# Attention walks: a written-out order of heads and steps for the first three and the last three walks, the periodic order only between them

## Time and profile before

| | |
|---|---|
| runs shown | 1484.58, 1487.13, 1488.78 us, median 1487.13 us |
| profiled execution | 1487.57 us, of it the span 1485.6 us |
| PE busy | 1411.2 us (95%), DVE 1124.7 (76%), ACT 1062.7 (72%), POOL 700.3 (47%) |
| granted PE clock, mean | 0.98 |
| chain that ended last | PE 87%, DVE 5%, issue 2%, ACT 2%, POOL 2%, DMA 2% |

### The profile page before, as it was taken

How to read it: one execution, slowest core, us unless ns; L and a number is a source line. 1 busy time by engine, 2 the same in 40 slices (tenths; PEclk the granted TensorE clock), 3 DMA queues, 4 the chain that set the end, 5 groups by cost and what they waited for, 6 DMA issues and landing times.

```text
span 1485.6 us, 38191 instructions
## 1 busy us (share of the span) xinstructions
PE 1411.2 (95%) x15004; PEld 1137.8 (77%) x15004; DVE 1124.7 (76%) x1991; ACT 1062.7 (72%) x2144; POOL 700.3 (47%) x619
## 2 busy tenths in 40 slices
PE   5689999999999999999999999999987999999996
PEld 3458888888888888898888889798874556767666
DVE  5578999999999999999999999999856621312215
ACT  6467878888787888878788887878654646465551
POOL 0535555455455555445554544555315535354440
PEclk9789999999999999999999999999998999999998
DMA  3000102021110202111020212202042111212100
GB/s 117 1 1 24 39 22 58 9 52 30 30 37 24 58 8 53 27 34 37 23 58 2 59 23 38 37 24 44 9 107 47 54 36 37 72 36 72 36 1 29
DMA packets 100999, 55.90 MB, mean 38 GB/s; under 512 B 74572, under 2 KB 93016, under 8 KB 100824
## 3 DMA queue, kind: packets, MB, share of 16 engines
q1 hardware_dynamic: 100824, 53.47, 15.1%
HBM read 35.62 MB, written 1.05 MB: 25 GB/s over the span
## 4 chain that ended last, share of the span: by engine, by line
PE 87%; DVE 5%; issue 2%; ACT 2%; POOL 2%; DMA 2%; POOLq 0%; SPq 0%; DVEq 0%; ACTq 0%
PE bank L387 11%; PE bank L1341 11%; PE bank L1324 10%; PE bank L542 6%; PE bank L588 5%; PE bank L529 5%; PE bank L559 4%; PE bank L577 4%; PE bank L568 3%; PE bank L469 3%; PE bank L477 3%; PE bank L485 3%; PE bank L437 2%; PE bank L413 2%; PE bank L438 2%
## 5 line engine op out<-in xcount | busy, mean ns | idle before, releaser
L878 DVE SCALAR_TENSOR_TENSOR con<-bank,taps,con 128x1022 f32<-128x1022 f32 (+2 forms) x192 | 245.2, 1277 | 13.2 <-ACT con L657 8.6
L1663 POOL TENSOR_TENSOR h<-h 128x512 f16<-128x512 f32 x120 | 142.5, 1192 | 159.8 <-ACT h L1441 147.4
L1034 POOL TENSOR_TENSOR gl<-const_sb,gc 128x512 f16<-128x512 f32 x128 | 129.7, 1040 | 141.7 <-DVE gc L888 84.3
L387 PE MATMUL bank<-x,qkv 128*128 128x512 f16 x768 | 184.6, 392 | 10.5 <-DVE con L878 10.2
L1440 ACT ACTIVATE h<-bank,b 128x512 f32<-128x512 f32 x120 | 82.5, 688 | 119.2 <-PE bank L1324 116.2
L1324 PE MATMUL bank<-y,w 128*128 128x512 f16 x720 | 162.8, 385 | 1.9 <-ACT h L1441 1.4
L1341 PE MATMUL bank<-w,h 128*128 128x256 f16 x1440 | 160.0, 273 | 0.0
L1341 PEld LDWEIGHTS bank<-w,h 128*128 128x128 f16 x1440 | 140.8, 98 | 18.5
L387 PEld LDWEIGHTS bank<-x,qkv 128*128 128x128 f16 x768 | 73.3, 100 | 93.1 <-issue 12.9
L936 DVE TENSOR_TENSOR X<-X,bank 128x512 f16<-128x512 f16 x192 | 129.3, 680 | 14.4 <-PE bank L477 12.7
L1324 PEld LDWEIGHTS bank<-y,w 128*128 128x128 f16 x720 | 70.1, 99 | 90.5 <-ACT h L1441 8.2
(11 more groups left out here) (221 smaller groups left out, 3927.8 us busy)
## 6 DMA issues: line engine op xcount, KB each, us to landing
w<-in_w SPq DMA_DIRECT2D x24, 640.0 KB, 4.5
w_qkv<-in_W_qkvz SPq DMA_DIRECT2D x16, 512.0 KB, 3.9
w_z<-in_W_qkvz SPq DMA_DIRECT2D x16, 256.0 KB, 2.8
w_out<-in_W_out SPq DMA_DIRECT2D x16, 256.0 KB, 3.0
Z<-in_xT SPq DMA_DIRECT2D x2, 512.0 KB, 5.4
y<-in_x SPq DMA_DIRECT2D x1, 1024.0 KB, 7.8
sqo<-oo SPq DMA_TRANSPOSE x64, 3.1
out_dram<-y SPq DMA_DIRECT2D x8, 128.0 KB, 1.8
```

Source lines behind the costliest of these rows:

```text
L387: last = mm(bank[:, b], qkv16[:, w, a, t * P:(t + 1) * P], x16[:, x, a, b * S:(b + 1) * S], start=(a == k == 0), stop=(a == HT - 1 and k = ...
L878: stt(out=out, in0=bank[:, 0:B, 0:S - k], scalar=taps[:, par, t, TAPS - 1 - k:TAPS - k], in1=out, op0=ALU.mult, op1=ALU.add).then_inc(tap_ ...
L1034: last = tt(gl[:, g % 2, k].rearrange("p (m r) d -> p m r d", m=2), upper.unsqueeze(1).unsqueeze(1).broadcast_to([P, 2, R, P]), gc[:, par, ...
L1663: tt(h16[:, n % 2, 1, t, at], h32[:, k % H32], h16[:, n % 2, 0, t, at], ALU.subtract).then_inc(h_low, 1)
```

## The change

The walks -2, -1 and 0 become one written list `FIRST` of 306 entries (head, step, x), the walks 13, 14 and 15 one written list `LAST` of 370. Between them walks 1 to 12 (`MIDDLE`) stay as they were. Both lists hold the same entries as the walks that they replace: no step is added or dropped, only the order differs. `steps_of` with its special case is gone, `run` goes through one list `STEPS`, and `place` looks up the use's number in it. The banks of `BANK` stay, but the order of the uses of a bank follows the lists. The banks in which the gate matmuls work change from (4, 2) to (3, 2).

```diff
-GATE_BANKS = (4, 2)
+GATE_BANKS = (3, 2)
+FIRST = [
+    (0, "load", "qkv"), (0, "split", "qkv"), (0, "proj", 1), (0, "tap", 1),
+    (0, "load", "out"), (0, "silu", 1), (0, "tap", 2), (0, "tok", 0),
+    (0, "tok", 1), (0, "proj", 2), (0, "tap", 3), (0, "sq1", 1),
+    (0, "gc", 0), (0, "proj", 3), (0, "kT", 0), (0, "gl", 0),
+    (0, "silu", 2), (0, "gl", 1), (0, "v", (0, 1)), (0, "v", (0, 0)),
+    (0, "tap", 0), (0, "silu", 3), (1, "load", "qkv"), (0, "proj", 0),
+    (0, "decay", 0), (0, "kd", 0), (0, "silu", 0), (0, "decay", 1),
+    (0, "kk", 0), (0, "sq", 0), (0, "gl", 2), (0, "aT", 0),
+    (0, "kk", 1), (0, "kT", 1), (0, "gl", 3), (0, "aH", 0),
+    (0, "aT", 1), (0, "aH", 1), (0, "kk", 2), (0, "st", 0),
...
+    (1, "silu", 1), (0, "split", "out"), (0, "norm", 0), (1, "proj", 2),
...
+    (0, "res", 0), (0, "y", (5, 1)), (1, "v", (0, 0)), (0, "split", "z"),
+    (1, "silu", 3), (1, "proj", 0), (0, "p", (5, 1)), (1, "tap", 0),
+    (0, "once", 0), (0, "res", 1), (0, "turn", (5, 1)), (1, "gl", 3),
+    (0, "res", 2), (0, "Z", 0), (0, "once", 2), (0, "once", 1),
+    (2, "load", "qkv"), (1, "load", "z"), (1, "silu", 0), (0, "res", 3),
+    (1, "decay", 1), (1, "v", (1, 1)), (1, "kk", 0), (1, "aT", 0),
...
+LAST = [
...
+    (14, "z", 1), (14, "weigh", 0), (15, "y", (4, 1)), (14, "high", 0),
+    (14, "weigh", 1), (15, "pT", 3), (15, "p", (5, 0)), (15, "v", (1, 0)),
+    (15, "turn", (3, 1)), (14, "z", 2), (15, "p", (4, 1)), (14, "high", 1),
+    (14, "z", 3), (14, "weigh", 2), (15, "y", (5, 1)), (15, "turn", (4, 1)),
+    (15, "turn", (5, 0)), (15, "res", 0), (14, "high", 2), (15, "p", (5, 1)),
+    (15, "res", 1), (15, "once", 0), (14, "op", 0), (15, "once", 1),
+    (15, "turn", (5, 1)), (15, "Z", 0), (14, "weigh", 3), (14, "oT", 3),
+    (15, "oT", 0), (14, "high", 3), (15, "res", 2), (14, "power", 0),
+    (15, "oT", 1), (14, "op", 1), (14, "low", 0), (15, "once", 2),
+    (14, "op", 2), (15, "Z", 2), (14, "low", 1), (15, "Z", 1),
+    (15, "kd", 1), (15, "oT", 2), (15, "solve", 0), (14, "op", 3),
+    (15, "su", 0), (15, "res", 3), (15, "ks", 1), (15, "pdl", 0),
+    (15, "solve", 1), (15, "qs", 1), (15, "su", 1), (15, "once", 3),
+    (15, "pdl", 1), (15, "sqo", 0), (15, "sqo", 1), (15, "sum", 0),
+    (15, "ks", 2), (14, "low", 2), (15, "split", "out"), (15, "Z", 3),
...
+MIDDLE = range(1, NK - 3)
+STEPS = FIRST + [(w + a, step, x) for w in MIDDLE for a, step, x in ORDER if 0 <= w + a < NK] + LAST
+USES = {b: [(n, step, x) for n, step, x in STEPS if BANK.get((step, x)) == b] for b in range(2, 8)}
+PLACE = {use: (b, k) for b in range(2, 8) for k, use in enumerate(USES[b])}
```

More of the change, by code:

```diff
@@ L106 @@
 }
-GATE_BANKS = (4, 2)
-DEEP = max(a for a, *_ in ORDER)
-AHEAD = {(step, x): a for a, step, x in ORDER}
-TILES = (1, 2, 3, 0)
[L115 to L130, removed]
@@ L131 @@
-STARTS = {(b, w): sum(len(USES[b, i]) for i in range(-DEEP, w)) for b in range(2, 8) for w in range(-DEEP, NK)}
-def place(n, step, x):
[L136 to L140, removed]
+GATE_BANKS = (3, 2)
[7 more added lines that the diff above has]
+    (0, "decay", 0), (0, "kd", 0), (0, "silu", 0), (0, "decay", 1),
[14 rows of a table added]
+    (0, "turn", (1, 1)), (1, "proj", 1), (0, "p", (2, 1)), (0, "turn", (3, 0)),
+    (0, "y", (4, 0)), (1, "tap", 1), (0, "turn", (2, 1)), (1, "gl", 1),
+    (1, "gl", 2), (1, "decay", 0), (0, "p", (4, 0)), (0, "y", (3, 1)),
+    (1, "silu", 1), (0, "split", "out"), (0, "norm", 0), (1, "proj", 2),
+    (0, "y", (5, 0)), (0, "p", (3, 1)), (1, "sq1", 1), (1, "tap", 2),
+    (1, "tok", 0), (1, "tok", 1), (0, "pT", 3), (1, "load", "out"),
+    (0, "turn", (4, 0)), (0, "aL", 2), (0, "turn", (3, 1)), (1, "silu", 2),
[4 rows of a table added]
+    (1, "silu", 3), (1, "proj", 0), (0, "p", (5, 1)), (1, "tap", 0),
+    (0, "once", 0), (0, "res", 1), (0, "turn", (5, 1)), (1, "gl", 3),
+    (0, "res", 2), (0, "Z", 0), (0, "once", 2), (0, "once", 1),
+    (2, "load", "qkv"), (1, "load", "z"), (1, "silu", 0), (0, "res", 3),
[10 rows of a table added]
+    (0, "pdl", 1), (1, "aL", 1), (1, "turn", (0, 0)), (0, "sqo", 0),
[8 rows of a table added]
+    (1, "y", (2, 1)), (0, "sum", 1), (1, "turn", (1, 1)), (0, "sqo", 2),
+    (2, "gl", 0), (2, "proj", 1), (1, "p", (2, 1)), (1, "turn", (3, 0)),
+    (2, "decay", 0), (2, "tap", 1), (1, "y", (4, 0)), (0, "solve", 3),
+    (2, "gl", 1), (0, "sum", 2), (2, "silu", 1), (1, "aL", 2),
+    (1, "norm", 0), (1, "aL", 3), (1, "pT", 3), (1, "kd", 0),
+    (0, "pdl", 3), (1, "turn", (2, 1)), (0, "sqo", 3), (1, "y", (3, 1)),
+    (1, "p", (4, 0)), (2, "proj", 2), (0, "sum", 3), (0, "power", 0),
+    (2, "sq1", 1), (1, "y", (5, 0)), (1, "p", (3, 1)), (2, "tap", 2),
+    (0, "weigh", 0), (2, "tok", 0), (2, "tok", 1), (1, "turn", (3, 1)),
[5 rows of a table added]
+    (1, "y", (5, 1)), (0, "high", 1), (1, "turn", (4, 1)), (1, "turn", (5, 0)),
+    (1, "res", 0), (0, "op", 0), (1, "once", 0), (0, "high", 2),
+    (0, "low", 0), (2, "v", (0, 0)), (2, "proj", 0), (0, "low", 1),
+    (1, "p", (5, 1)), (2, "tap", 0), (0, "high", 3), (2, "silu", 3),
+    (1, "res", 1), (0, "op", 1), (1, "turn", (5, 1)), (1, "res", 2),
+    (0, "low", 2), (1, "Z", 0), (0, "low", 3), (0, "oT", 3),
+    (1, "once", 2), (0, "op", 2), (2, "silu", 0), (2, "gl", 2),
+    (2, "decay", 1), (0, "op", 3),
+]
@@ L143, in after @@
+MIDDLE = range(1, NK - 3)
+TILES = (1, 2, 3, 0)
+STEPS = FIRST + [(w + a, step, x) for w in MIDDLE for a, step, x in ORDER if 0 <= w + a < NK] + LAST
+USES = {b: [(n, step, x) for n, step, x in STEPS if BANK.get((step, x)) == b] for b in range(2, 8)}
+PLACE = {use: (b, k) for b in range(2, 8) for k, use in enumerate(USES[b])}
+def place(n, step, x):
+    return PLACE[n, step, x]
 def after(n, k):
[L144 removed]
+    return n >= k
 def attention(nc, ins, y_tok, const, ones, ident16, bank, sb, sem, experts):
@@ L241, in latest @@
             back = back[0] if back else 0
[L242 to L245, removed]
+            if after(n, back):
+                b, k = place(n - back, step, x)
+                if b != besides:
+                    last[b] = max(last.get(b, 0), k)
+        return list(last.items())
     def is_full(eng, n, *uses):
@@ L272, in run @@
     def run(eng, todo, then={}):
[L274 to L279, removed]
+        for n, step, x in STEPS:
+            if step in todo:
+                todo[step](n, n % 2, x)
+                if n == 0 and (step, x) in then:
+                    then[step, x]()
     def sync(sp):
```

37 lines of the change are left out of this document (added), and 78 rows, old and new, of tables (FIRST, LAST).

## The result

The kernel before took 1486.20 us (median of five runs, 1484.26 to 1488.78), the changed kernel 1480.46 us (five runs, 1478.91 to 1483.97). The ratio is 0.9963, with a 95% interval of 0.9952 to 0.9974: some 5.5 us faster. In a later group of runs on one chip it was 0.9952 [0.9938, 0.9967].

A forecast was written before the change was run, and what follows sets the result against it. PE was taken as full in the middle walks, with gains only in the first 113 us and the 102 us from 1030.82; 4.9 + 1.4 + 2.3 + 0.4 = 9.0 us off 1487.57 gave 1478.6 us, range 1472.5 to 1485.

The forecast's parts named there:

- The early gates: Head 0's front: `gc` at 38.7 instead of 48.28, first `kk` at 48.6 instead of 53.48; main part of 4.9 us.
- The earlier taps: Head 0's front: `tap` 0 ends at 47.4 instead of 48.4, within the gain of 4.9 us.
- (2): Head 0: `proj` 3 ends at 32.6, its copies precede silu 2 and gate powers, `tap` 3 starts at 33.3 instead of 35.28.
- steps (3) and (4): Head 0: ACT finishes gate powers at 38.7, then v copies, silu 3 and `proj` 0's copies by 43.5; `tap` 0 ends at 47.4.
- Step (1): Head 0: `tok` (1.04 us) goes before `proj` 2, which takes 4.44; `proj` 3 starts at 29.8, 0.8 us later.
- The table loads: Two added ACT loads of 1.28 us ahead of head 0's silu 0 are hidden by `tap` 0, ready at 47.2.
- From `st` to head 1's `kk`: Stretch from head 0's `st` to head 1's first `kk` stays 53.4 us; clock bounds: 2.5 gained, 1.7 lost.
- more: the clock: Rival, front: fewer holes keep PE at 2.4 GHz in one more `proj` block, gain 11.5 us, 1476.1; chance 0.13.
- The hole ahead of head 1's `kk`: PE's idle 1.04 + 1.12 us there gets filled by `once` 1, `res` 3, `v` (1, 1): 1.4 us, 0 to 2.2.
- slower: a full walk is opened: Rival, walks 0 and 13: new PE waits make one walk 16.3 us longer, 1494.9; chance 0.11.
- Walk 14: Moving `weigh` 3, `op` 3, `res` 3 later and `Z` 1 earlier around head 15's `solve` 0 wins 2.3 us, 0 to 3.4.
- less: the end gives nothing: Rival: the front gives back some and the end wins nothing, gain 4.0 us, 1483.6; chance 0.18.

The follow-up runs named there:

- tok back: Changed kernel with `once` 1, `res` 3, `v` (1, 1) behind head 1's first `kk` and `tok` behind `proj` 2: ratio 0.9959 to the kernel before.
- the kernel without the fillers: Changed kernel with `once` 1, `res` 3 and `v` (1, 1) moved behind head 1's first `kk`: ratio 0.9956 to the kernel before.
- decay 0 late: Changed kernel with head 0's `decay` 0 moved behind `silu` 0, `gc` and `gl` still early: ratio 0.9974 to the kernel before.
- the early gates in the periodic order: Kernel before with only head 0's `gc` and `gl` moved ahead of `proj` 0, `decay` still last: ratio 0.9945, again 0.9966.

## Why the prediction was right, and where it was not

1478.6 us was forecast, 1480.46 measured; the sum was 9.0 us and the profile gave 7.1 (1487.57 - 1480.46), the medians of all runs 6.3. Part of the nearness is luck: the sum was taken from one execution, 1.4 us above the median of 1486.20. Taken from the median it gives 1477.2, 3.3 us below what was measured.

*The early gates: right, and nearly all of the gain.* The step "kk 0 at 48.6 instead of 53.48" rested on `gc` at 38.7 and on silu 0 as the next late thing. `gc` came at 40.32, and `kk` began 0.1 us behind the end of silu 0. A is 1.19 in all eleven profiles with `gc` and `gl` early, 5.11 in both with the old first walks: 3.92 us. Putting them back undid the ratio, with 1.0 us of `kd` beside it.

*The earlier taps: wrong.* Of the 4.9 us, 1.0 was to come from `tap` 0 ending at 47.4 instead of 48.4. It ended at 48.73, so that the first `kk` gained 3.56 us, less than my lower bound of 4.3. The step that failed is (2), "`proj` 3 ends at 29.8 + 2.76 = 32.6". It took 4.44, the bound that I had named, and the gate powers ended at 40.3, not 38.7. What the bound left out is ACT: behind them it ran v, a table load, silu 3 and the copies without a gap, and finished the copies for `tap` 0 at 44.79. ACT, not PE, set `tap` 0: `proj` 0, at the full clock (2.76), was done at 42.02, 1.5 us before ACT came to its copies. In the prediction's own steps (3) and (4) a later `proj` 3 goes through ACT undiminished, so the bound for 4.44 should have been 4.9 - 1.7 = 3.2, not 4.3. Step (1) was off too, `tok` took 1.94 instead of 1.04, but `proj` 2 took 3.41 instead of 4.44. And 0.35 us arose ahead of the first `tap`, which began at 14.98 instead of 14.63 (13.94 to 15.97 over the fourteen profiles). Counted from its start `tap` 0 ended after 33.76 us, and after 33.74 before: the gain is 0.0. Over all profiles this distance is 33.73 to 35.26 in the periodic order and 33.52 to 34.91 in the written one (32.52 with tok back), so that nothing speaks for a gain here.

*The table loads: right.* They were ready at 48.54, 0.2 us ahead of `tap` 0's end, the margin that the prediction had. Each took 1.28 us, and the ACTIVATE behind it started 0.01 to 0.02 us later. By the 2.66 us per switch of the Trainium skill ("ScalarE: Activation LUTs", "What ACT_TABLE_LOAD costs") silu 0 would have been about 2.5 us late, by an estimate from that figure; the trace disagrees.

*From `st` to head 1's `kk`: the size was off.* I left it at 53.4 with an upper bound of 2.5 for the clock. It was 49.96, 3.45 less, and the kernel without the fillers has the same, so they are no part of it. The clock is most of it: head 1's stretch had 0.95 instead of 0.86, the `proj` that took 5.30 at the earlier trace rows took 4.24, and PE's busy time from `st` to `kk` fell from 42.15 to 39.97 us although 23 more matmuls ran there (519 against 496). So the rival "more: the clock" was partly right beside the forecast: the granted clock rose. Its reason, that bursts behind idle gaps keep starting at half clock (the Trainium skill, "TensorE: Matmul & The Clock Gate", "HAM oscillation — how this bites in real kernels"), fits the hole that shrank, but no run here isolates it. Whether the early gates cause it stays open. Within the periodic order they go together: C is 53.41 in both profiles with late gates, at a granted clock of 0.84, and 49.4 to 51.1 in all four with early ones, at 0.93 to 0.97, with 490 to 492 matmuls each time. Within the written order they don't: the one profile with late gates has 50.96, and of the seven with early ones six have 49.96 to 50.93 and decay 0 late has 54.15.

*The hole ahead of head 1's `kk`: right as a term, but paid back.* Forecast 1.4, and 1.18 by the pair of kernels. But walk 0, put at 0 "and only a loss is possible", lost more. The same matmuls between the two `kk` take 65.45 us in the periodic order and 67.15 in the written one without the fillers: 1.70 us in pieces of up to 0.3. PE's waits in walk 0 of the changed kernel:

```profile
PE bank L632 <- DVE Y L1082: 0.3, 1, 0.3
PE bank L640 <- DVE X L1091: 0.2, 1, 0.2
PE bank L684 <- ACT Z L881: 0.2, 1, 0.2
```

In the periodic walk none of these is listed. Of the 1.70 us PE is idle for 0.8; 0.9 lie inside what counts as busy, 0.33 of it at `y` and the rest in small pieces over many steps (walk 0 of before, then of the kernel without the fillers):

```profile
113.43:178.88 65.45, 65.33 (x792) 56.24 (x793) 61.18 (x108) 54.20 (x116) 34.14 (x31) 1.00 0.15 34
```

```profile
105.04:172.19 67.15, 66.25 (x792) 56.02 (x793) 59.86 (x106) 53.09 (x114) 33.38 (x32) 1.00 0.11 17
```

That is the rival "slower: a full walk is opened", with a price of 1.7 instead of 16.3 us. Net, the written walk 0 and the fillers cost 0.5.

Walk 13 lost as much, unseen. The prediction said that it "has the same work"; in fact `op` 3 of head 13 and `once` 2 of head 14 leave it for walk 14, 16 matmuls that take some 1.5 us. The walk took 65.30 us instead of 65.38 (before, then after):

```profile
965.44:1030.82 65.38, 65.26 (x794) 56.17 (x793) 61.86 (x108) 52.81 (x114) 33.45 (x30) 1.00 0.16 34
958.08:1023.38 65.30, 64.24 (x778) 54.48 (x777) 60.70 (x108) 51.67 (x115) 34.16 (x31) 1.00 0.17 34
```

All ten profiles with a written list at the end have 65.28 to 65.30 here, the four with the periodic one 65.38 or 65.39. PE's idle time rose from 0.12 to 1.06 us, and the other half microsecond lies again inside what counts as busy.

*Walk 14: wrong.* Forecast 2.3, and 0.6 lost in the profile, 58.02 to 58.63. The step that failed is "net 1.2", and with it "together 2.6". `op` 3 of head 14 and `res` 3 did leave the stretch from `kk` of head 15 to its `solve` 0, but beside `Z` 1 the two steps from walk 13 came into it, which the prediction didn't count: PE starts 756 matmuls there where it had 748. The relief of 1.2 us holds only for walks 13 and 14 together, and they took 123.93 us instead of 123.40 (122.25 in the second profile of the changed kernel). Beside this, DVE's `weigh` 2 takes 2.56 us, and took 1.72 before (the row of 2.77 in the earlier trace rows is `weigh` 2 and 3). Two rows of DVE after:

```profile
1069.54 2.56 DVE L1153 SCALAR_TENSOR_TENSOR oo<-oo,rso,zs 128x128 f32<-128x128 f32 x4
1072.02 0.68 DVE L1082 TENSOR_TENSOR Y<-bank,ymask 128x512 f16<-128x512 f32 x1
```

and PE, which needs that Y, waits:

```profile
1072.75 0.41 PE L632 MATMUL bank<-Y,Z 128*128 128x64 f16 x8 [1.54 <-DVE Y L1082]
```

This wait is there in the second profile of the changed kernel too, whose E is 56.97, so it is no reason to be slower than before. What makes the difference between the two is the clock. With the written list as it is, E has two values, 57.0 (four profiles) and 58.6 (five). In all five the `z` matmuls that begin 37.5 us behind `kk` ran partly at half clock (`z` 0 took 2.75 us in four, 2.04 in one with 2.40 for the next), in none of the four (1.48). The same stretch of two executions of the changed kernel, cut at `z` 0 and ahead of it:

```profile
1060.80:1063.60 2.80, 2.80 (x24) 2.00 (x20) 1.01 (x2) 0.00 (x0) 2.13 (x1) 0.51 0.03 6
1051.00:1060.80 9.80, 8.90 (x144) 8.26 (x141) 9.57 (x21) 6.23 (x12) 3.26 (x4) 1.00 0.01 2
```

```profile
1064.50:1066.10 1.60, 1.60 (x28) 1.46 (x25) 1.00 (x2) 0.05 (x1) 1.60 (x1) 1.00 0.04 10
1054.70:1064.50 9.80, 8.90 (x144) 8.26 (x141) 9.57 (x21) 6.23 (x12) 3.25 (x4) 1.00 0.01 2
```

What PE did in the 9.80 us before is the same in both, down to the busy time, and then one had the full clock and the other half of it. In the four profiles with the periodic list E is 57.4 to 58.0. So the written list wins 0.4 to 1.0 us in this stretch where the clock stays and loses 0.6 to 1.2 where it doesn't; the forecast's rival "less: the end gives nothing" was right for this part.

*The chain of head 15: wrong by its small size.* 0.4 forecast, F went from 44.71 to 44.92.

So the sum came near by errors of opposite sign. Walk 14 gave 2.9 us less than forecast, the fillers with walk 0 1.9, the taps with the later start 1.4, the chain 0.6: 6.8 less. The stretch up to head 1's `kk` gave 3.45 that I had only as a bound, above its upper end of 2.5, and 1.2 came from `kk` to `st`, the middle walks, walk 13 and the experts (0.13, 0.75, 0.08, 0.27), where E's spread of 1.6 within one list shows that such sizes mean nothing. 9.0 - 6.8 + 3.45 + 1.2 = 6.85, and the span is 6.9 shorter. That the total came so near is luck. The forecast of the sign, and its main term, rest on the gates alone.

No version beats the changed kernel measurably. The one to keep is the early gates in the periodic order: the same time, as far as these runs can tell (1481.63 against 1480.20 us on one chip, with intervals that overlap), from a change of four lines.

## What to carry to other kernels

When a cheap step (here a copy of 0.20 us) stands in an engine's queue behind long work that it doesn't need, and another engine idles until it runs, move that step by itself and measure before writing out an order: that move was the gain here, to within the 2 us that the runs resolve. A written order in a walk that one engine already filled lost 1.7 us here and some 1.5 in a second walk, in pieces too small for a list of waits to stand out; the distance between two events that enclose the same instructions shows it. When steps are moved past the event that ends a stretch, list also what comes in past the event that begins it. Judge an item of 1 us by such distances over several profiles, never by one: the clock alone moved one stretch by 1.6 us.

## What the runs showed of the hardware

- The same work of PE was followed by different granted clocks. Seven profiles with this last list have the same 492 matmuls in the 37.5 us from `kk` of head 15 to `z` 0, each within 0.02 us of its place in the profile of the changed kernel. `z` 0 then took 1.48 us in four of them and 2.75, 2.75 and 2.04 in three. For two executions of one kernel the rows above have 1.00 and 0.51 for the next stretch; 0.51 is the level of 1.2 GHz.
- DVE's SCALAR_TENSOR_TENSOR on 128 x 128 f32, all operands in SBUF, takes 0.34 us, and 1.13 us for four. When it starts while POOL's TENSOR_TENSOR (also in SBUF) runs, it ends 0.15 us behind POOL's end. For `weigh` 2 after, this happened twice, with `low` and `kd`: DVE's first two instructions took 0.99 and 1.13 us, hence 2.56 for four. POOL in that stretch:

```profile
1069.22 1.16 POOL L1224 TENSOR_TENSOR oo<-oo 128x512 f16<-128x512 f32 x1 [1.21 <-ACT oo L940]
1070.33 1.09 POOL L1216 TENSOR_TENSOR kd<-k_tok,gc 128x512 f32<-128x512 f32 x1
```

It was so in all nine profiles with this list as it is. In the kernel before, the group of four at 1070.73, with POOL idle, took 1.14, and the one at 1072.90, beside `low` from 1072.61 to 1073.76, 1.80. All 13 instructions of this line that took longer than 0.4 us in the profiles before and after end 0.145 to 0.152 us behind a POOL instruction. One that starts 0.03 us before POOL's isn't delayed. DVE's operations with an operand in PSUM don't wait: the 47 readouts of `y` that lie wholly inside such a POOL instruction in the profile after took 0.68 us, as the others do.
